# Experts' gate and up products with the weights stationary, copied per tile by VectorE, and eight buffers for rows and results

## The reference, cut to what matters

```python
x = L0_attn_x                      # 4 x 1024 x 256, float32
xn = _layernorm(x)
x = x + _L0_attn_ref(xn, ...) + _L0_ffn_ref(xn, ...)

# _L0_ffn_ref: two of E = 8 experts for each of 4096 tokens, F = H = 256
sorted_xs = x_flat[xs_indices, :]                       # 8192 rows, by expert
gate_out = ragged_dot(sorted_xs, w_gate, group_sizes=tokens_per_expert)   # (8192, 2 * 256)
activation = gelu(gate_out[:, 0, :]) * gate_out[:, 1, :]
expert_outputs = ragged_dot(activation, linear, group_sizes=tokens_per_expert)
out = sum over the two choices of combine_weight * per_expert_scale * expert_outputs
```

## Time and profile before

| what | value |
|---|---|
| three runs | 894.17, 894.63 and 898.16 us, median 894.63 us |
| the profiled execution's own time | 894.28 us |
| its span | 892.5 us |
| `experts`, first gather to last scatter | 590.3 to 827.0 us of the span |
| TensorE busy | 816.1 us |
| mean granted clock of TensorE | 0.965 |

### The profile page before, as it was taken

The page is one execution under the profiler, slowest core; times in us unless marked ns, Lnnn a source line. Parts: engine busy times, 40 slices in busy tenths (PEclk is TensorE's granted clock), DMA queues, the critical chain, the costliest instruction groups (busy, mean ns, idle before and its releaser), DMA issues. The chain is left out here.

```text
span 892.5 us, 17183 instructions
## 1 busy us (share of the span) xinstructions
PE 816.1 (91%) x5618; PEld 422.1 (47%) x5619; DVE 555.9 (62%) x1560; ACT 491.2 (55%) x1011; POOL 397.1 (44%) x478
## 2 busy tenths in 40 slices
PE   4999878999998999999999999849999999999598
PEld 2555413334443344444444444315556555565597
DVE  4777399999999988888888887002222222222287
ACT  1444303777776777777877777823333333333374
POOL 6666301111211245433555421234666666665397
PEclk9999957999999999999999999969999999999699
DMA  8899767766535775567665500056222222222485
GB/s 195 275 290 279 248 84 94 90 72 84 65 50 59 85 100 84 84 87 110 85 91 84 70 2 7 1 169 226 83 86 84 82 83 87 82 85 68 143 251 186
DMA packets 93631, 100.25 MB, mean 112 GB/s; under 512 B 32700, under 2 KB 74300, under 8 KB 93500
## 3 DMA queue, kind: packets, MB, share of 16 engines
q1 hardware_dynamic: 84600, 80.40, 45.8%
q0 software_dynamic: 8960, 18.95, 6.8%
HBM read 63.89 MB, written 35.00 MB: 111 GB/s over the span
## 5 line engine op out<-in xcount | busy, mean ns | idle before, releaser
L825 ACT ACTIVATE probs<-spsum 128x512 f32<-128x512 f32 x576 | 317.5, 602 | 145.1 <-PE spsum L898 138.3
L664 DVE CUSTOM_DVE_ANT_0 junk<-mpsum,mask 128x128 bf16<-128x128 f32 (+7 forms) x512 | 359.1, 754 | 45.3 <-issue 29.6
L872 PE MATMUL mpsum<-ks,qs 102*128 102x512 bf16 (+3 forms) x768 | 183.7, 343 | 28.6 <-DVE maxima L664 22.0
L898 PE MATMUL spsum<-qs,ks 105*128 105x512 bf16 (+3 forms) x768 | 198.1, 329 | 4.8 <-ACT probs L825 3.4
L644 POOL TENSOR_SCALAR_AFFINE_SELECT probs<-probs 128x512 f32<-128x512 f32 x128 | 79.2, 638 | 252.6 <-ACT probs L825 252.3
L918 PE MATMUL cpsum<-probs,vs 128*17 128x256 f32 (+2 forms) x2560 | 154.0, 361 | 1.5 <-POOL probs L644 0.8
L1100 PE MATMUL gu<-w_gu,xTs 128*128 x288 | 137.4, 600 | 1.7 <-ACT xTs L1044 1.7
L1079 DVE COPY hT<-hp 128x256 f32<-128x256 f32 x72 | 30.6, 425 | 165.8 <-PE hp L1107 165.8
L872 PEld LDWEIGHTS mpsum<-ks,qs 102*128 102x128 bf16 x768 | 67.5, 100 | 111.7 <-DVE maxima L664 55.4
L898 PEld LDWEIGHTS spsum<-qs,ks 105*128 105x128 bf16 x768 | 66.9, 97 | 90.8 <-ACT probs L825 39.2
L1019 POOL DMA_INDIRECT expert_rows<-y,places x72 | 70.8, 984 | 69.9 <-ACT y L1053 69.6
(11 more groups left out here) (122 smaller groups left out, 708.5 us busy)
## 6 DMA issues: line engine op xcount, KB each, us to landing
qk_parts<-ctxT SPq DMA_DIRECT2D x32, 384.0 KB, 3.6
qs<-qk_parts SPq DMA_DIRECT2D x96, 128.0 KB
ks<-qk_parts SPq DMA_DIRECT2D x96, 128.0 KB
yk<-expert_rows SPq DMA_DIRECT2D x32, 256.0 KB, 3.0
v_rows<-ctxT SPq DMA_DIRECT2D x8, 544.0 KB, 3.6
vs<-v_rows SPq DMA_DIRECT2D x16, 272.0 KB, 11.0
ctxT<-in_x SPq DMA_DIRECT2D x8, 512.0 KB, 6.2
xn_rows<-ctxT SPq DMA_DIRECT2D x8, 512.0 KB, 5.7
```

The costliest lines, as they stand in the source:

```text
L664: last = dve.tensor_tensor_reduce(junk[:, slot, c:c + w], mpsum[:, slot, c:c + w], keep["mask"][:, S - w:S], 1.0, 3 * NEG, ALU.add, ALU.ma ...
L825: act.activation(probs[:, u % PRING, h], spsum[:, SCORE_AT["S", n, h] % SRING], ACT.Exp, scale=SCALE).then_inc(exp_done, 1)
L872: last = pe.matmul(mpsum[:, slot, at + c:at + e], qs[hq][0:R_MAX, h, qt * P:(qt + 1) * P], ks[hq][0:R_MAX, h, c:e], start=True, stop=True)
L898: last = pe.matmul(spsum[:, SCORE_AT["S", n, h] % SRING, c:c + w], ks[hq][:, h, kt * P:(kt + 1) * P], qs[hq][:, h, q0:q0 + w], start=True, ...
```

## The change

`gate_up` is turned round: the expert's weights are stationary, in 128x128 pieces, and `xTs` streams past them, 128 columns at a time, so that `gu` comes out with hidden units as its partitions. Four output pieces by two halves of the contraction are eight matmuls in place of two. The product of gate and up is then already `hT`, and `hid`, `hp`, `hidden_T` and VectorE's copy of `hp` fall away. The stationary pieces are read from `w_now`, a double buffer of 128 x 1024 elements, into which VectorE copies the expert's weights for tile s + 2 behind its product of tile s. RR goes from 4 to 8. The loops are written out (no `Fori`), `down` runs one tile behind `gate_up` in place of three, and TensorE reads one expert number a tile.

```diff
-    RR = 4
+    RR = 8
...
-        hid = sb("hid", [P, 2, HID])
+        w_now = sb("w_now", [P, 2, DH, 2 * HID])
...
+            xT_copy(0)
+            xT_copy(1)
+            for s in range(NST):
+                gelu(s)
+                if s + 2 < NST:
+                    xT_copy(s + 2)
+                if s >= 1:
+                    store(s - 1)
+            store(NST - 1)
...
         @block.vector
         def _(dve):
-            def body(s, par, i):
+            def weights(s):
+
+                e = dve.value_load(keep["tile_expert"][0:1, s:s + 1], min_val=0, max_val=NE - 1)
+                dve.tensor_copy(w_now[:, s % 2].rearrange("p a c -> p (a c)"), w_gu[:, ds(e * DH, DH)].rearrange("p a c -> p (a c)")).then_inc(w_ready, 1)
+
+            dve.wait_ge(keep["w_gu_in"], 16 * NE)
+            weights(0)
+            weights(1)
+            for s in range(NST):
                 dve.wait_ge(gate_ready, s + 1)
-                dve.tensor_tensor(hid[:, par], gu[:, par, HID:2 * HID], gate[:, par], ALU.mult).then_inc(hid_ready, 1)
-                dve.wait_ge(hp_ready, s + 1)
-                dve.tensor_copy(hT[:, par].rearrange("p a t -> p (a t)"), hp[:, par, 0:HID]).then_inc(hT_ready, 1)
-
-            tiles(dve, body)
+                dve.tensor_tensor(hT[:, s % 2].rearrange("p a t -> p (a t)"), gu[:, s % 2, HID:2 * HID], gate[:, s % 2], ALU.mult).then_inc(hT_ready, 1)
+                if s + 2 < NST:
+                    weights(s + 2)
...
-            def gate_up(s, par, e):
+            def gate_up(s):
+
                 pe.wait_ge(xT_ready, s + 1)
+                pe.wait_ge(w_ready, s + 1)
+                for c in range(2 * HID // P):
+                    for dh in range(DH):
+                        last = pe.matmul(gu[:, s % 2, P * c:P * (c + 1)], w_now[:, s % 2, dh, P * c:P * (c + 1)],
+                                         xT[:, s % 2, dh], start=dh == 0, stop=dh == DH - 1)
+                last.then_inc(gu_ready, 1)
+
+            def down(s, e):
+                pe.wait_ge(hT_ready, s + 1)
+                if s >= 2:
+                    pe.wait_ge(y_ready, s - 1)
                 for dh in range(DH):
-                    last = pe.matmul(gu[:, par], xT[:, par, dh], w_gu[:, ds(e * DH + dh, 1)].rearrange("p a c -> p (a c)"),
-                                     start=dh == 0, stop=dh == DH - 1)
-                last.then_inc(gu_ready, 1)
...
+            rows_T(0)
+            rows_T(1)
+            going = expert_of(0)
+            for s in range(NST):
+                gate_up(s)
+                if s + 2 < NST:
+                    rows_T(s + 2)
+                if s == 1:
+                    pe.wait_ge(w_in, 16 * NE)
+                if s >= 1:
+                    down(s - 1, going)
+                    going = expert_of(s)
+            down(NST - 1, going)
```

More of the change, by code:

```diff
@@ L978, in experts @@
         gu = ctx.enter_context(nc.psum_tensor("gu", [P, 2, CH], F32))
-        hp = ctx.enter_context(nc.psum_tensor("hp", [P, 2, CH], F32))
         yp = ctx.enter_context(nc.psum_tensor("yp", [P, 2, CH], F32))
@@ L985, in experts @@
         tp_ready, xT_ready = sem("tps_ready"), sem("xTs_ready")
-        gu_ready, gate_ready, hid_ready = sem("gu_ready"), sem("gate_ready"), sem("hid_ready")
-        hp_ready, hT_ready = sem("hp_ready"), sem("hT_ready")
+        gu_ready, gate_ready, hT_ready, w_ready = sem("gu_ready"), sem("gate_ready"), sem("hT_ready"), sem("w_now_ready")
         yp_ready, y_ready = sem("yp_ready"), sem("y_ready")
         block = ctx.enter_context(nc.Block())
[L991 to L995, removed]
         @block.sync
@@ L1040, in _, with xT_copy, gelu @@
         def _(act):
-            def xT_copy(s, par):
+            def xT_copy(s):
                 act.wait_ge(tp_ready, s + 1)
-                act.activation(xT[:, par].rearrange("p a t -> p (a t)"), tp[:, par, 0:D], ACT.Copy).then_inc(xT_ready, 1)
-            def gelu(s, par):
+                act.activation(xT[:, s % 2].rearrange("p a t -> p (a t)"), tp[:, s % 2, 0:D], ACT.Copy).then_inc(xT_ready, 1)
+            def gelu(s):
                 act.wait_ge(gu_ready, s + 1)
-                act.activation(gate[:, par], gu[:, par, 0:HID], ACT.Gelu_apprx_tanh).then_inc(gate_ready, 1)
@@ L1050, in store @@
-            def store(s, m):
+                act.activation(gate[:, s % 2], gu[:, s % 2, 0:HID], ACT.Gelu_apprx_tanh).then_inc(gate_ready, 1)
+            def store(s):
                 act.wait_ge(yp_ready, s + 1)
                 act.wait_ge(y_free, s + 1)
[L1053 to L1071, removed]
+                act.activation(y[:, s % RR], yp[:, s % 2, 0:D], ACT.Copy).then_inc(y_ready, 1)
+            xT_copy(0)
[6 more added lines that the diff above has]
+                    store(s - 1)
@@ L1083, in _, with rows_T @@
+                if s + 2 < NST:
+                    weights(s + 2)
         @block.tensor
         def _(pe):
-            pe.wait_ge(keep["w_gu_in"], 16 * NE)
-            def rows_T(s, m, i):
-                pe.wait_ge(rows_in[m], 16 * (i + 1))
+            def rows_T(s):
+                pe.wait_ge(rows_in[s % RR], 16 * (s // RR + 1))
                 for dh in range(DH):
-                    last = pe.transpose(tp[:, m % 2, dh * P:(dh + 1) * P], rows[:, m, dh * P:(dh + 1) * P], keep["ident"][:, :])
+                    last = pe.transpose(tp[:, s % 2, dh * P:(dh + 1) * P], rows[:, s % RR, dh * P:(dh + 1) * P], keep["ident"][:, :])
@@ L1092, in rows_T @@
                 last.then_inc(tp_ready, 1)
             def expert_of(s):
-                return pe.value_load(keep["tile_expert"][0:1, ds(s, 1)], min_val=0, max_val=NE - 1)
-            def gate_up(s, par, e):
+                return pe.value_load(keep["tile_expert"][0:1, s:s + 1], min_val=0, max_val=NE - 1)
+            def gate_up(s):
                 pe.wait_ge(xT_ready, s + 1)
-                for dh in range(DH):
-                    last = pe.matmul(gu[:, par], xT[:, par, dh], w_gu[:, ds(e * DH + dh, 1)].rearrange("p a c -> p (a c)"),
-                                     start=dh == 0, stop=dh == DH - 1)
-                last.then_inc(gu_ready, 1)
@@ new lines, in gate_up @@
+                for c in range(2 * HID // P):
[7 more added lines that the diff above has]
+                    pe.wait_ge(y_ready, s - 1)
+                for dh in range(DH):
+                    last = pe.matmul(yp[:, s % 2, 0:D], hT[:, s % 2, dh], w_down[:, ds(e * DH + dh, 1)].rearrange("p a c -> p (a c)"),
```

## The result

In the first measurement the changed kernel takes a median of 881.36 us (four runs, 878.63 to 881.89) where the kernel before takes 894.45 (894.17 to 898.16). The ratio is 0.984, with an interval of 0.981 to 0.987. The forecast was 875. Measured once more, on the chip of the last group of experiments, it comes out the other way: 912.67 for 903.41 us, ratio 1.011 (1.008 to 1.013). First the profile of the run of 878.63 us.

A forecast was written before the change was run, and what follows sets the result against it. TensorE was taken to bound `experts`: down(0) at 603.2, 71 periods of 2.83 and about 0.25 us put down(71) at 804.4, against 823.96 before. That is 19.6 us off 894.28: 874.7, forecast 875 us, range 869 to 907.

The forecast's parts named there:

- The bound and the period: In `experts` TensorE's own work sets the pace: 2.83 us a tile, 0.27 less than 3.104.
- rival A: In gate and up, weight loads bound the 16 pairs: 911 us at 0.14 a pair, 968 at 0.19; chance 0.20.
- Loops written out: In `experts`, 17 times round the loop lose 0.34 us each, so writing them out saves 5.7 us.
- The copy: VectorE's copy of 1024 weight elements a tile takes 0.71 us, 1.21 at the upper price, hidden within 2.83.
- rival B: GpSimd becomes the bound, its DMA issues and VectorE's copy excluding each other: 883 to 904 us; chance 0.20.
- rival C: VectorE's register load, behind the wait for `hT`, is exposed by 0.2 us a tile: 889 us; chance 0.08.
- The start: At the start of `experts`, down(0) comes at 603.2 instead of 607.02; the wait for `w_down` costs nothing.
- The end: At the end of `experts`, down(71) comes at 804.4, with about 0.25 us for the last `hT`; the rest is unchanged.

The follow-up runs named there:

- e9: The changed kernel unaltered, measured again on the chip of the last group: 912.67 us, ratio 1.011 to the kernel before.
- e5: The changed kernel with gate and up matmuls streaming 64 columns in place of 128 from tile 2 on, same weight loads: 917.52 us, ratio 1.015.
- e1: The kernel before with its loops in `experts` written out on TensorE, ScalarE and VectorE, nothing else: 895.68 us, ratio 0.992.
- run 69: Not a run label: in "In the same run 69 issues begin amid a copy", 69 counts DMA issues in the changed kernel's run of 878.63 us.
- e4: The changed kernel with VectorE's weight copy made twice, the second into a buffer nobody reads: 907.71 us, ratio 1.007.
- e6: The changed kernel with SyncE waiting for the rows of tile 2 before it issues `w_down`: 909.49 us, ratio 1.008.
- e3: The changed kernel without VectorE's copy, stationary pieces read straight from `w_gu`: 912.00 us, ratio 1.011.
- e10: The changed kernel with `down` two tiles behind, rows turned three ahead, three buffers, gathers eight ahead, copy ahead of the product: 906.42 us, ratio 1.003.
- e2: The changed kernel with RR = 4: 910.02 us, ratio 1.009.
- e11: The changed kernel with ScalarE's order in `experts` as a loop over eight tiles in place of written out: 913.39 us, ratio 1.011.
- e12: The kernel before with loops written out and gate and up cut into matmuls of 128 columns, `xTs` still stationary: 930.79 us, ratio 1.030.

## Why the prediction was right, and where not

In the first measurement the time fell as forecast, by 15.7 us on the profiled executions (894.28 to 878.63) where the sum said 19.6. The reasons forecast are those that the trace shows. That the total came so near is in part luck, since errors cancel (the start and the end below), and that the sign held is luck too: this measurement had no late signals, and e9 had. Step by step:

**The bound and the period** hold: 2.871 for 2.83, which over 71 tiles makes 2.9 us of the miss. The pair costs 0.111 and not 0.109, 0.03 us a tile, and the rest is within the reading of the starts.

**Weight loads, rival A,** did not come. But e5 shows how near it was: a pair costs 0.110 with half the columns, so the pair's own price and the stream of 128 columns lie on each other. "At most 0.11 to 0.14" was the right reading of single loads, and its lower end was true. The Trainium skill ("TensorE: Matmul & The Clock Gate", Back-to-back issue gap) would have had pairs cost some 25 ns more than matmuls alone (81 for 56). For these float32 pairs the trace does not agree: 111 ns, beside half of the 0.215 us that `down`'s matmuls of 256 columns take.

**Loops written out:** 5.7 predicted, 6.1 by e1's profile.

**The copy** took 0.694 us for 0.71 and was hidden. **GpSimd, rival B:** its mechanism is real, its price was not. A DMA issue and the copy exclude each other for most of their length. In the tile shown first, the copy ends at 702.00, and the scatter, which begins at 701.66, ends at 702.86, 0.86 us later. In the same run 69 issues begin amid a copy, and 67 of them end 0.82 to 0.89 us after it, where an undisturbed one takes 0.96 to 0.99 in all; the other two began within 0.03 us of the copy's start and weren't held. A copy that begins 0.74 us into an issue takes up to 0.74 us itself (e9). The price came to 0.15 us a tile because the scatter mostly met the last 0.2 to 0.4 us of the copy. Where it meets nearly all of it, as in e9, it costs as much:

```profile
706.97 0.69 DVE L1062 COPY w_now<-w_gu 128x1024 f32 x1 [0.32 <-issue]
707.02 1.70 POOL L1011 DMA_INDIRECT expert_rows<-y,places  x1 [2.37 <-ACT y L1045]
...
707.92 0.68 DVE L1062 COPY w_now<-w_gu 128x1024 f32 x1
```

Two copies fall into this issue, and it takes 1.70 us for 0.99. Where the copies fall counts more than how much is copied: in e4, with twice the copying, the issues are hardly longer on average. The Trainium skill ("SBUF — State Buffer", SBUF: two separate sides) has such a copy lock GpSimd out of writing its descriptors; the traces agree. The tile of GpSimd came to about 2.7 us and still fitted.

**Register load, rival C:** VectorE sits idle 0.55 us on issue ahead of the copy, under cover.

**The start** is the step that failed. down(0) came at 607.50, not 603.2. Of the 4.3 us, 1.2 lie ahead of the first transposes (`attend` itself ended 1.0 later), and 0.7 in the first gate and up, which began 0.95 behind rows_T(1) and ran at half the clock for 3.55 us where I had 3.4. 1.7 are rows_T(1), at 599.83, 3.0 us behind rows_T(0) where I had 1.3; the two first gathers, beside VectorE's first two copies, took 1.19 and 1.16, and then waited for their data. The other 0.7 are the second gate and up, 2.75 us to `down` where I had 2.1: the granted clock is still 0.50 from 604 to 606 us, while before it was 1.00 from 602 us on. I had costed the loads of `w_down` at nothing because they were issued in time; e6 shows, for the later groups, that they and the rows share what bounds the start.

**The end:** I gave down(71) a whole period and 0.25 us behind down(70), 3.08, although only `hT` lies between them; it took 1.19. That is 1.9 us too much in my sum, and 19.6 - 2.9 - 4.3 + 1.9 = 14.3 is what the stage gave. Behind it the first `sumsT` came 8.60 us after the last `down` for 8.16 before (832.12 - 823.96), and from there to the end of the span are 58.5 us for 60.4. With these 1.5 it is the 15.7 measured, to 0.1.

**What I had not seen at all** is the room that the change gave up. `down` ran three tiles behind and runs one behind, and I checked only that `hT` is ready 1.9 us ahead of its use. That holds while TensorE's signals come at once. In the later groups they come up to some three us late about every third tile, ScalarE's work waits for them, and TensorE loses what goes over 1.9 (1.1 us a stop in e3): 912.67 us, outside my range. The semaphore times of e3 and e9 show that the signals are TensorE's, and e10 that room gives time back. Why they are late is not settled. It isn't the copy (e3), not RR (e2), not ScalarE's straight code alone (e11), not the short pairs alone (e12), and the kernel before with loops written out has none (e1). Whether they come with a rate of tiles under 3 us, or with the sum of all queues' instructions, was not tried. Nor is it known why the first measurement had none, or why `attend` is some 7 us longer in the others; the chip differed among the later groups without effect, and which one the first had isn't on record.

## What to carry to other kernels

Cut a period by counting TensorE's records, and leave the chain behind them the room it had: a consumer moved from three tiles behind to one is a cost that a quiet profile shows as zero. Time a change worth 1 to 2% on more than one chip before believing its sign; here it was 0.984 in one measurement and 1.011 in another, and only the loops written out (0.992) helped where the rest did not. When an engine sits idle and then runs several instructions on end, look at when its semaphore was raised, and at another engine that waits for the same one, before calling it the engine's own stop. When a start waits for data, look at every transfer in flight, not at who was issued first.

## What the hardware showed unexpectedly

- A pair of float32 weight load and matmul costs 0.110 us with 64 columns and 0.111 with 128, at a granted clock of 1.00.
- The same program takes 881 us in one measurement and 913 in another, at the same granted clock in `experts`; the kernel before 894 and 902 to 903.
- In the slower measurements TensorE's semaphores are raised up to three us behind the end of its records, in bursts of five within 0.3 us, at nearly equal distances (9.84 us in e3), while its next matmuls go on. In the first measurement none is late. ScalarE sits idle for 4.4 us there, and in e10 VectorE with it.
- A DMA issue on GpSimd that starts while a float32 copy of 0.69 us runs ends 0.82 to 0.89 us after the copy (undisturbed it takes 0.96 to 0.99 in all). One issue that met two copies took 1.70 us (e9).
- Behind matmuls with addresses from a register the next one comes some 0.34 us late (2.12 for 1.78 at the median, e12) after sixteen records of 0.11 each, and not after four of 0.43 (1.72, e1).
